# Four graph layers in one kernel: the transposed adjacency from 32 by 32 blocks and VectorE, the centering on GpSimd, and the stages of the graphs six steps apart

## The reference, cut to what matters

```python
h = relu(layernorm(x)); x = x + attention(h, adj)      # 4 heads, softmax over adj > 0.5
h = relu(layernorm(x)); x = x + relational(h, adj)     # max over 7 relations: adj, adj^T, shifts, eye
h = relu(layernorm(x)); x = x + convolution(h, adj)    # D^-1/2 (adj + I) D^-1/2 (h W^T + b), relu
h = relu(layernorm(x)); x = x + laplace(h, adj)        # inner layernorm, xn W_self + (I - S adj S) xn W_neigh, softplus
```

## Time and profile before

| | |
|---|---|
| time, median of 2 runs | 699.27 us (697.95 to 700.59) |
| the profiled execution's own time | 699.71 us |
| its span, first to last instruction | 697.7 us |
| PE (TensorE) busy | 648.7 us, 93% |
| ACT (ScalarE) busy | 544.8 us, 78% |
| DVE (VectorE) busy | 531.5 us, 76% |
| POOL (GpSimd) busy | 369.2 us, 53% |
| mean busy share of the DMA engines on SP's queue | 19.7% |
| one adjacency load (1 MB), issue to landing, median | 5.8 us |
| mean granted TensorE clock | 0.970 |

### The profile page before, as it was taken

One profiled execution on the slowest core, in us unless ns is written; L12 is line 12 of the kernel. 1 busy time (PEld: TensorE's weight loads), 2 busy tenths in 40 slices (PEclk: granted clock), 3 DMA queues, 4 the chain that ended last, 5 costly groups with the idle time before them and its releaser, 6 DMA issues. The chain is left out here.

```text
span 697.7 us, 20320 instructions
## 1 busy us (share of the span) xinstructions
PE 648.7 (93%) x7476; PEld 525.4 (75%) x7476; DVE 531.5 (76%) x1641; ACT 544.8 (78%) x1271; POOL 369.2 (53%) x435
## 2 busy tenths in 40 slices
PE   5669899999999999999999999999999899998855
PEld 4466778879697878788797878788796768787544
DVE  5776768887878788887878788887878778884641
ACT  5777668888888898888888897988888776865442
POOL 2545565564746565654846465655742564454420
PEclk9589999999999999999999999999999999999996
DMA  7222040222222111222222211222212210200000
GB/s 212 92 59 80 3 137 3 77 77 78 77 78 77 61 39 57 76 78 78 77 77 78 76 50 44 64 79 77 77 62 77 63 53 25 78 2 16 1 15 16
DMA packets 39532, 44.47 MB, mean 64 GB/s; under 512 B 4545, under 2 KB 23050, under 8 KB 39434
## 3 DMA queue, kind: packets, MB, share of 16 engines
q1 hardware_dynamic: 38802, 42.95, 19.7%
q10 hardware_dynamic: 632, 0.22, 0.1%
HBM read 38.83 MB, written 4.33 MB: 62 GB/s over the span
## 5 line engine op out<-in xcount | busy, mean ns | idle before, releaser
L475 POOL TENSOR_TENSOR rstd<-ve,half_neg 128x4 f32<-128x4 f32 (+1 forms) x67 | 89.1, 1329 | 208.1 <-DVE ve L1388 63.9
L797 ACT ACTIVATE side<-d_all,sd 128x512 bf16<-128x512 f32 x256 | 163.8, 713 | 35.3 <-DVE pos L1307 29.3
L1833 PEld LDWEIGHTS ps<-part,pos 128*128 128x128 bf16 x3072 | 101.3, 97 | 9.4 <-issue 6.1
L1833 PE MATMUL ps<-part,pos 128*128 128x66 bf16 x3072 | 103.4, 193 | 0.2 <-DVE pos L1307 0.2
L1307 DVE TENSOR_TENSOR pos<-side,none 128x2048 bf16<-128x2048 bf16 x64 | 80.7, 1260 | 6.1 <-ACT side L797 5.1
L1369 DVE TENSOR_REDUCE best<-ps 128x128 f32<-128x896 f32 x64 | 68.5, 1086 | 12.8 <-PE ps L1929 11.4
L2031 PE MATMUL ps<-u,adj_tr 128*128 128x128 f32 x512 | 62.5, 282 | 3.0 <-ACT u L897 3.0
L2031 PEld LDWEIGHTS ps<-u,adj_tr 128*128 128x128 f32 x512 | 60.6, 198 | 4.3 <-ACT u L897 4.3
L1819 PEld LDWEIGHTS ps<-part,nmask 128*128 128x128 bf16 x1536 | 53.4, 99 | 13.1 <-issue 12.9
L1877 PE MATMUL ps<-adj_tr,h 128*128 128x512 f32 x128 | 58.5, 600 | 0.2 <-ACT h L706 0.2
L1891 PE MATMUL ps<-adj_in,h 128*128 128x512 f32 x128 | 57.8, 593 | 0.0
(11 more groups left out here) (162 smaller groups left out, 1488.0 us busy)
## 6 DMA issues: line engine op xcount, KB each, us to landing
adj_in<-in_adj SPq DMA_DIRECT2D x16, 1024.0 KB, 5.8
d_all<-d_dram SPq DMA_DIRECT2D x64, 256.0 KB, 3.7
x_in<-in_x SPq DMA_DIRECT2D x16, 256.0 KB, 3.0
out_y<-y_out SPq DMA_DIRECT2D x15, 256.0 KB, 2.5
d_dram<-sd_t SPq DMA_DIRECT2D x64, 2.0 KB, 1.4
w_sb<-in_L_gnn_W SPq DMA_DIRECT2D x7, 64.0 KB, 2.2
b_sb<-in_L_gnn_b SPq DMA_DIRECT2D x1, 256.0 KB, 3.2
out_y<-y_out SPq DMA_DIRECT2D x2, 128.0 KB, 1.8
```

Source lines behind the costliest of these rows:

```text
L475: G.tensor_tensor(rstd[:, cut], ve[:, cut], half_neg[:, cut], ALU.pow).then_inc(power, 1)
L797: last = A.activation(side[:, t, :], d_all[:, h, :], ACT.Sign, bias=sd[:, 0, h, t:t + 1])
L1833: last = mm(ps[:, B_HEADS[q] + i // 2, o:o + VAL], pos[h % 2][:, t, i * P:(i + 1) * P], parts[n][:, t, h, :], start=False, stop=(i % 2 == ...
```

## The change

The TensorE pieces `adjacency(t)` and their ScalarE copies go. In their place SP loads the adjacency a second time into `adj_blk`, so that a 32-row band of a tile holds the blocks of adj already at their mirrored places; each contiguous run is 32 numbers, 128 bytes. VectorE then turns each 32 by 32 block in place of its own, four instructions of 128 by 512. ScalarE takes the sums over `adj_tr` in four instructions of their own. `adj_blk` is a single buffer.

The centering moves from VectorE's `norm3` to GpSimd's `center`, and the rest of `norm3` becomes `norm4`. `DEPTH` is 7, all lists are in another order, and banks and bank waits are assigned anew. `r2`, `gl`, `z` share one tile with two setup tiles. `first_data` is gone, `load_weights` is later in SP's list.

```diff
-DEPTH = 9
+DEPTH = 7
+            def load_blocks(g):
+                if g.has(1):
+                    sync.wait_ge(adj_sb, g.before(1).all(1))
+                for b in range(T):
+                    for t in range(T):
+                        lo = t * P + b * (P // T)
+                        sync.dma_start(adj_blk[b * (P // T):(b + 1) * (P // T), t, :].rearrange("r (m c) -> r m c", c=P // T),
+                                       adj[g.n, :, lo:lo + P // T].rearrange("(m r) c -> r m c", r=P // T)
+                                       ).then_inc(s_blk, 16)
 # SP, start: load_features(0), load_features(1), load_blocks(0), scores_out(0), load_features(2),
 #   scores_in((0,))(0), load_adjacency(0), scores_in((1,2,3))(0), load_blocks(1), load_adjacency(1),
 #   load_laplace, load_blocks(2), load_edge_rows, scores_out(1), scores_in(1), load_weights, ...
+            for s in range(6, GRAPHS + DEPTH - 1 - 6):          # SP
+                scores_in((0,))(at(s - 3))
+                scores_in((1, 2, 3))(at(s - 3))
+                store(at(s - 6))
+                load_blocks(at(s - 2))
+                load_adjacency(at(s - 2))
+                load_features(at(s))
+                scores_out(at(s - 2))
+            def center(g):                                      # GpSimd
+                pool.wait_ge(bn3, g.all(3))
...
+                for t in g.tiles:
+                    last = G.tensor_scalar(gl[:, t, :], x3[:, t, :], mv3[:, t, 0:1], 0.0, ALU.subtract, ALU.max)
+                last.then_inc(cen3, 1)
+            def column_sums(g):                                 # ScalarE
+                act.wait_ge(adj_sb, g.all(1))
...
+                for t in range(T):
+                    last = A.activation(junk[:, t, :], adj_tr[g.three][:, t, :], ACT.Copy,
+                                        accum_out=sums[g.three][:, 0, t:t + 1])
+                last.then_inc(col_sum, 1)
+            def adjacency(g):                                   # VectorE
+                dve.wait_ge(s_blk, g.all(16 * T * T))
...
+                for t in range(T):
+                    last = V.transpose(adj_tr[g.three][:, t, :], adj_blk[:, t, :])
+                last.then_inc(adj_sb, 1)
 # VectorE, loop: degrees(s-3), part_rest(s-3), largest(0)(s-4), norm4(s-5), part_lo(s-3),
 #   largest(1)(s-4), head(1)(s-3), largest(2), largest(3), residual1(s-4), head(2)(s-3), norm2(s-4),
 #   pair(0)(s-3), head(3)(s-3), scores(s-2), pair(1)(s-3), attention(s-3), residual0(s-3), norm1(s-3),
 #   norm0(s), laplace(s-5), top_score(s-2), adjacency(s-2), weights(s-2), no_edges(s-2), softplus(s-5),
 #   edges_negative(s-2), head(0)(s-2), residual2(s-4), node_scales(s-3), norm3(s-4)
 # TensorE, loop: h1_transposed(s-4), product_ah(s-4), product_ath(s-4), h0_transposed(s-2),
 #   relation(0), (1), (2)(s-4), no_edges(0)(s-3), relation(3)(s-4), head(0)(s-3), row_sums(s-3),
 #   project(s-2), head(1)(s-3), no_edges(1)(s-3), z_transposed(s-5), head(2)(s-3), mean_value(s-2),
 #   head(3)(s-3), h2_transposed(s-4), laplace_linear(s-5), conv_bias, conv_linear(s-4),
 #   laplace_product(s-5), top_rows(s-2), conv_product(s-4), top_all(s-2)
 # ScalarE, loop: normal3(s-5), sums_across(s-3), sides(3)(s-3), z_transposed(s-5), hidden2(s-4),
 #   row_sums(s-2), h2_transposed(s-4), laplace_in(s-5), projected(s-2), conv_in(s-4), laplace_own(s-5),
 #   sides(0)(s-2), hidden1(s-3), softplus(s-5), weights(s-2), conv_relu(s-4), column_sums(s-2),
 #   h1_transposed, product_ah, product_ath(s-3), part_hi(s-2), h0_transposed(s-1), low_weights(s-2),
 #   part_mid(s-2), sides(1)(s-2), hidden0(s), sides(2)(s-2)
```

More of the change, by code:

```diff
@@ L1046, in _ @@
-            h1_transposed(at(12))
+            hidden1(at(2))
+            softplus(at(0))
+            sides(0)(at(3))
+            conv_relu(at(1))
+            h1_transposed(at(2))
+            weights(at(3))
+            column_sums(at(3))
+            product_ah(at(2))
+            product_ath(at(2))
+            part_hi(at(3))
+            part_mid(at(3))
+            sides(1)(at(3))
+            hidden0(at(5))
+            h0_transposed(at(4))
+            sides(2)(at(3))
+            low_weights(at(3))
@@ L1504, in _ @@
             norm1(at(0))
+            top_score(at(1))
+            norm0(at(2))
+            weights(at(1))
+            bias_rows()
+            edge_parts()
             node_scales(at(0))
-            top_score(at(1))
-            weights(at(1))
+            degrees(at(1))
+            part_rest(at(1))
             no_edges(at(1))
+            adjacency(at(2))
+            edges_negative(at(1))
+            largest(0)(at(0))
             head(0)(at(1))
-            edges_negative(at(1))
-            norm0(at(4))
@@ L1591, in _ @@
-            node_scales(at(12))
+            residual2(at(0))
+            norm3(at(0))
+            norm0(at(4))
+            part_rest(at(2))
+            norm4(at(0))
+            head(0)(at(2))
+            largest(0)(at(1))
+            part_lo(at(2))
+            largest(1)(at(1))
+            head(1)(at(2))
+            largest(2)(at(1))
+            largest(3)(at(1))
+            head(2)(at(2))
+            residual1(at(1))
+            norm2(at(1))
+            head(3)(at(2))
+            pair(0)(at(2))
@@ L1604, in _ @@
[L1604 to L1608 removed]
             residual1(at(12))
             norm2(at(12))
+            head(3)(at(13))
+            pair(0)(at(13))
+            scores(at(14))
             pair(1)(at(13))
@@ L2071, in _ @@
[L2071 to L2084 removed]
+            h1_transposed(at(0))
+            product_ath(at(0))
```

1172 lines of the change are left out of this document (544 added, 628 removed).

## The result

The changed kernel takes 726.77 us (725.31 to 728.23, 2 runs) where the one before takes 699.27: a ratio of 1.0393, 95% interval 1.027 to 1.0516. It is slower, and outside the range that was forecast. The profiled execution took 728.23 us, its span is 726.4 (697.7 before).

The account below looks back on a forecast made before the run. TensorE's own list bounds the kernel before; after the change, a loop through VectorE. Fill 127 + 10 x 37.6 + 112.5 + 70.6 = 686.1 us of span, with 2.0 around it 688; range 667 to 712.

Parts of the forecast that it names:

- the loop through VectorE: TensorE from `no_edges(0)` to `top_all`, 23.4 us, then VectorE until the next `no_edges(0)`, 14.2: a turn of 37.6 us.
- the walk of the fill: Start to graph 2's fourth head, with weight loads late in SP's queue: 127 us, 6.7 more than before.
- the drain: From graph 12's fourth head to graph 15's: 118.1 less three times 1.9, 112.5 us; the last 70.6 kept.
- What bounds before: In a loop turn of the kernel before, TensorE is busy all 38.88 us; its own list is the bound.
- What goes from TensorE: Four groups of four transposes, 0.47 us each, leave its list: 1.9 us a turn, leaving 37.0.
- VectorE's part of the loop: VectorE's work after `top_all`, from `weights` to `part_lo`, before TensorE's next `no_edges(0)`: 14.2 us, using durations of before.
- The wait of `relation(0)`: TensorE waits about 0.3 us a turn for the copy of `product_ath`, with only `h0_transposed` between.
- B: TensorE stays full, both waits overrated: 16 x 1.9 = 30 us off, 670 (665 to 676); chance 0.20.
- C: VectorE's transposes between `top_score` and `weights` outgrow their cover, from 0.63 us each; at 1.1, 713 us; chance 0.08.
- D: The block load's 128-byte packets are slow: at 53 ns each, 27 us, turn grows by 5, 753 us; chance 0.12.
- E: GpSimd's `center` holds VectorE up, by up to 2.15 us; with 1.3 the turn is 38.9: 705 us; chance 0.16.

Follow-up runs that it names:

- experiment 8: Kernel before, with TensorE transposing one adjacency block of four from graph 3 on (transposed adjacency wrong): 691.97 us, 0.9883; turn 38.07.
- experiment 6: Changed kernel, `part_lo` earlier in VectorE's turns: ahead of `largest(0)` 735.84 us; right behind it 728.12 (turn 40.24); the latter with reordered fill 715.97.
- experiment 1: Changed kernel with the fill reordered: SyncE loads weights before scores, edge rows and blocks, VectorE splits edge rows sooner: 713.33 us, 1.0201.
- experiment 3: Changed kernel with VectorE transposing one block row of four from graph 3 on: 727.56 us, 1.0398; turn 40.05.
- experiment 4: Changed kernel with each block load reading whole 2 KB rows instead of 128-byte pieces (transposed adjacency wrong): 726.38 us, 1.0385; turn 40.03.
- first kernel of experiment 9: Kernel before, nine steps deep, with only the exchange: block load, VectorE transposes, ScalarE column sums, centering on VectorE: 779.54 us, 1.1156; turn 44.19.
- first kernel of experiment 7: Changed kernel with reordered fill and a new loop order (scales, degrees, `part_rest` before `residual2`, `part_lo` before `largest(0)`): 743.92 us, 1.0649.

## Why the prediction was wrong

Three terms of the sum failed, and their errors add up: the loop through VectorE (14.2 us put, 15.56 measured, with 1.0 more on TensorE's side of it: 37.6 put for the turn, 40.0 measured, 25 us over ten turns), the walk of the fill (127 put, 137.2 measured) and the drain (112.5 put, 118.2 measured).

**What bounds before: right.** TensorE's list does; experiment 8 shows it, and that other pauses take over soon, 0.81 us paid for 1.29.

**What goes from TensorE: nearly right.** Its list was put at 37.0; it is 37.76 busy, and 24.4 instead of 23.4 from `no_edges(0)` to `top_all`. Of this 1.0, 0.31 is the wait for `h2t`, which the walk did not have. Some 0.46 are short pauses: laid start beside start with the turn before, five other pieces take 0.05 to 0.13 us longer and the bias 0.07, and one 0.08 less. The rest is rounding in the walk's terms. Ten turns: some 10 us.

**VectorE's part of the loop: the failed step, mis-sized.** 14.2 forecast, 15.56 measured. The walk took durations of before into a neighbourhood that had changed. Three instructions came out at 2.30, 1.56 and 1.03 where the rows of before have 1.23, 0.83 and 0.15: +2.7. The stretch of `degrees` was shorter than before, 1.23 for 2.78, since its two long sums no longer lie beside GpSimd's `val`: -1.55. The wait for `center` is 0.3. Together +1.4. The mechanism (this loop, PE waiting for `part_lo` ahead of `no_edges(0)`) was right, its sum 2.4 us a turn too short. It isn't the only chain of that length, which the walk did not see: in experiment 6 this wait went and the turn stayed at 40.2.

**The wait of `relation(0)`: right**, 0.3 forecast and 0.55 measured, in no sum.

**The fill: the second failed step, right in kind, 10 us short.** The order of the queue was read rightly, and experiment 1 shows it. The terms failed one by one: 16 block issues took 8.30 us, not 7.2; the edge rows began at 58.90, not 54.7, because VectorE's `edge_parts` began 2.7 us later than walked and took 5.0 us, not 3.5; the relation started at 79.97, not 73.5. From there graph 1's head came at 98.4 (18.4 later, 18 put), graph 2's 38.8 after that, not 35.5, with 5.2 us of waits of TensorE between, the longest 1.56 for the largest score, where about 2 were put.

**The drain: the third failed step.** It was credited with 3 x 1.9 us for a shorter list of TensorE. But its turns took 40.1, 39.6 and 38.5, the first with the waits of the loop, the other two with short ones (the longest 1.0 us, for ScalarE's `u`). TensorE's busy time there fell by 2.2 us, from 114.4 to 112.2, and its idle time rose by as much. It came out at 118.2, as before. This contradicts the forecast's own argument, which had just said that the list isn't the bound any more.

**The rivals.** B would need the loop below TensorE's list: it is 2.3 above. C: a transpose costs 0.62 us, just under the 0.63 from which C was to decide, and experiment 3 excludes it. D: experiment 4 excludes it; the issue of 16 loads took 8.5 to 9.6 us in the ten turns, and VectorE never waits for a block. E was right in kind and wrong in place: not `center`, but `val` and `y_out`, which the change did not touch, only brought beside other VectorE work. Its price was 1.3 us on the loop; the lengthening was 2.7, of which the shorter `degrees` hid 1.55. Without the fill's 16.9 us the change would be at about 710; E gave 705, and that nearness is luck.

**What no experiment settled:** whether an order exists in which the exchange pays, at either depth. TensorE's 1.9 us a turn are real, as far as experiment 8 shows; none of nine hand-made orders with all the work in them reached a turn under 39.3.

## What to carry over

When work moves off the engine that is full, close the loops between the engines with durations measured in the new neighbourhood, or bound each VectorE instruction by its longest length in the trace and not by its usual one: the trace of before has the comparison once at 2.16 us and the first scale at 1.23, outside the ten turns. A loop of which the longest lengths overshoot the old turn is a risk to be priced. Walk each issue queue in the fill in order: putting the weights behind the blocks and the edge rows cost 13.4 us here, as much as the ten turns lost. And credit the drain only with what its own bound allows.

## What the runs showed of the hardware

**VectorE beside GpSimd.** A VectorE instruction with two tensor inputs from SBUF that starts while GpSimd works on one with two wide inputs takes its own length and nearly the rest of GpSimd's. In the turn shown the comparison starts 1.21 us before the end of `y_out` and is 1.07 us longer than alone (2.30 for 1.23). The sum of `residual2` starts 1.01 before the end of the first `val` and is 0.87 longer (1.56 for 0.69), and the first scale, 128x4, starts 1.01 before the end of the second and is 0.88 longer (1.03 for 0.15). Beside `adj_own`, whose instructions are short, with 0.42 and 0.29 us left, it is 0.28 and 0.14. The added time goes by what is left of the GpSimd instruction, not by the size of VectorE's. GpSimd's get longer too: two of `val` take 3.54 us where they took 2.12 before. VectorE instructions with one input kept their length beside the same ones: the mask beside `y_out` 0.69, a transpose beside `val` 0.67, statistics 0.28 and maxima 1.08 each. `center`, a GpSimd operation with one tensor and one scalar per partition, added 0.13 us at most to an instruction of `degrees` and next to nothing to `part_rest` (1.26 for 1.25); it was itself lengthened beside `part_rest`, 1.51 for 0.71. GpSimd's small powers (128x12, 2.29 us) added nothing. The Trainium skill (SBUF — State Buffer, SBUF: two separate sides) says that whichever of the two starts first holds the shared ports for its whole instruction, and on VectorE's side counts operations with two SBUF inputs, or in a mode that takes both ports, among those that do. The rests above agree for `val`, `y_out` and `adj_own`. The Trainium skill makes no exception there for a GpSimd operation like `center` or the powers; on these the measurement decides.

**The block load** in 128-byte runs lands 2.5 us after issue (median), in 2 KB rows 2.0, and the turn is the same. The factor of 19 that the prediction quotes from the Trainium skill for a strided copy does not appear.

**TensorE after a long wait.** In the first kernel of experiment 9 the product that follows a 3.2 us wait takes 5.40 us for its eight matmuls, not the 3.60 of the earlier trace rows. The timeline of PE, then windows of PE alone (length, busy, granted clock, DMA):

```profile
381.81 5.40 PE L1862 MATMUL ps<-adj_tr,h 128*128 128x512 f32 x8 [3.19 <-ACT h L723]
```
```profile
381.81:387.21 5.40, 5.40 (x10) 0.68 0.77 121
378.60:381.80 3.20, 0.02 (x1) 1.00 0.54 85
...
387.20:391.00 3.80, 3.80 (x15) 1.00 0.40 96
```

The granted clock is 1.00 (2.4 GHz) up to the end of the wait, 0.68 in the product behind it, a mean of that level and of 1.2 GHz, and 1.00 again after it. So this wait cost 1.8 us beside its own 3.2, in every turn in which it stood. In the first kernel of experiment 7 a wait of 2.4 us was enough in some turns: the 48 products behind it took 2.48 us there and not 1.66, and these turns are the ones of 43.6 us among those of 42.0. The changed kernel's longest wait in a turn, 1.41, left the clock at 1.00.
